# Grouped attention: key blocks stored and loaded by SyncE, both halves in one DMA, and the first turn's operands made ready during the projections

## The reference

```python
q = (hidden_states @ Wq.T)...                    # 32 heads of 128, rotated
k_r0 = hidden_states @ Wkr.T                     # rotary half of the keys
c_kv = hidden_states @ Wdk.T                     # latents
k_c = c_kv @ Wupk.T                              # other half of the keys
v = (c_kv @ Wupv.T).reshape(bsz, q_len, KV_HEADS, HEAD_DIM)
...
attn = jax.nn.softmax(scores, axis=-1)           # causal
out = jnp.einsum('bhqk,bhkd->bhqd', attn, v)
return out.reshape(...) @ Wo.T
```

## Time and profile before

| | us |
|---|---|
| median of 3 runs (2343.11 to 2350.22) | 2343.27 |
| the profiled execution, device time | 2351.52 |
| its span, first to last instruction | 2349.8 |
| TensorE busy | 2125.6 (90%) |
| VectorE busy | 1406.4 (60%) |
| ScalarE busy | 1082.5 (46%) |
| GpSimd busy | 835.4 (36%) |

### The profile page before, as it was taken

The page is one execution under the profiler, slowest core; times in us unless marked ns, Lnnn a source line. Parts: engine busy times, 40 slices in busy tenths (PEclk is TensorE's granted clock), DMA queues, the critical chain, the costliest instruction groups (busy, mean ns, idle before and its releaser), DMA issues. The chain is left out here.

```text
span 2349.8 us, 33208 instructions
## 1 busy us (share of the span) xinstructions
PE 2125.6 (90%) x11408; PEld 1456.4 (62%) x11408; DVE 1406.4 (60%) x2597; ACT 1082.5 (46%) x2627; POOL 835.4 (36%) x1060
## 2 busy tenths in 40 slices
PE   5999988878999999999997879999999986899988
PEld 3333356656777777777765656777777674554457
DVE  5788464326656566556554636666666555657756
ACT  4677543214444444444443635555555433335553
POOL 0000101545344444444431035455555313246621
PEclk8999888989999999999999979999999987989999
DMA  3000022751011111111011144444333201543310
GB/s 112 1 1 1 4 90 84 153 128 41 25 53 37 36 54 32 41 54 32 23 41 36 62 103 108 108 108 105 88 98 78 61 23 58 160 91 68 72 33 37
DMA packets 113587, 149.48 MB, mean 64 GB/s; under 512 B 40127, under 2 KB 53567, under 8 KB 111246
## 3 DMA queue, kind: packets, MB, share of 16 engines
q1 hardware_dynamic: 65422, 109.08, 16.4%
q0 software_dynamic: 48000, 38.28, 7.1%
HBM read 86.39 MB, written 27.26 MB: 48 GB/s over the span
## 5 line engine op out<-in xcount | busy, mean ns | idle before, releaser
L1851 POOL TENSOR_TENSOR attn0b_probs<-attn0b_probs,attn0b_recip 128x128 f32<-128x128 f32 (+3 forms) x256 | 192.4, 772 | 223.4 <-DVE attn0b_recip L2090 223.3
L2482 POOL TENSOR_TENSOR attn1a_probs<-attn1a_probs,attn1a_recip 128x128 f32<-128x128 f32 (+3 forms) x256 | 178.9, 720 | 234.8 <-DVE attn1a_recip L2665 234.2
L2538 ACT ACTIVATE attn1a_probs<-attn1a_scores,attn1a_negmax 128x128 f32<-128x128 f32 (+3 forms) x256 | 132.7, 523 | 175.4 <-DVE attn1a_negmax L2651 174.2
L1957 ACT ACTIVATE attn0b_probs<-attn0b_scores,attn0b_negmax 128x128 f32<-128x128 f32 (+3 forms) x256 | 132.6, 523 | 150.0 <-DVE attn0b_negmax L2083 148.8
L1965 ACT ACTIVATE attn0b_probsT<-attn0b_turned 128x128 f32<-128x128 f32 (+3 forms) x128 | 56.0, 437 | 243.3 <-PE attn0b_turned L2231 242.9
L2244 PE MATMUL attn0b_out<-attn0b_probsT,attn0b_v_now 128*128 128x512 f32 x320 | 153.9, 612 | 11.4 <-DVE attn0b_probsT L2097 11.4
L1440 DVE TENSOR_REDUCE attn0a_negmax<-attn0a_by_query 128x2 f32<-128x1024 f32 x128 | 151.9, 1219 | 11.7 <-PE attn0a_by_query L1557 11.7
L2651 DVE TENSOR_REDUCE attn1a_negmax<-attn1a_scores 128x2 f32<-128x256 f32 (+3 forms) x128 | 105.4, 824 | 71.4 <-PE attn1a_scores L2840 71.4
L2083 DVE TENSOR_REDUCE attn0b_negmax<-attn0b_scores 128x2 f32<-128x256 f32 (+3 forms) x128 | 104.8, 819 | 46.9 <-PE attn0b_scores L2220 46.9
L37 PE MATMUL attn0b_aux<-attn0b_wo_hi,attn0b_oT_hi 128*128 128x512 f32 x256 | 125.6, 490 | 1.4 <-DVE attn0b_oT_lo L2101 1.4
L2852 PE MATMUL attn1a_turned<-ident_f,attn1a_probs 128*128 128x128 f32 x640 | 116.1, 280 | 8.7 <-DVE attn1a_probsT L2659 7.3
(11 more groups left out here) (507 smaller groups left out, 6121.2 us busy)
## 6 DMA issues: line engine op xcount, KB each, us to landing
pre<-in_b_o SPq DMA_DIRECT2D x16, 1024.0 KB, 5.3
attn1a_qT<-attn1a_stage SPq DMA_DIRECT2D x128, 128.0 KB, 2.4
attn1a_qT<-attn1a_stage SPq DMA_DIRECT2D x64, 256.0 KB, 3.8
pre<-in_b_q SPq DMA_DIRECT2D x8, 1024.0 KB, 6.1
pre<-in_b_kv SPq DMA_DIRECT2D x5, 1024.0 KB, 7.1
attn0b_vals<-attn0b_v_out SPq DMA_DIRECT2D x16, 256.0 KB, 5.0
attn0b_keys_hi<-attn0b_part_hi POOLq DMA_DIRECT2D x32, 128.0 KB, 4.9
attn0b_keys_lo<-attn0b_part_lo POOLq DMA_DIRECT2D x32, 128.0 KB, 7.6
```

What stands on the lines that cost most here:

```text
L1851: pool.tensor_tensor(x, x, recip[:, r % 2, e:e + 1].broadcast_to([P, (qt + 1) * P]), ALU.mult).then_inc(s_scaled, 1)
L1957: act.activation(probs[:, r % 2, e, 0:width], scores[r % 2][:, e, 0:width], ACT.Exp, bias=negmax[:, r % 2, e:e + 1], accum_out=sums[:, r % ...
L2482: pool.tensor_tensor(x, x, recip[:, r % DEEP, e:e + 1].broadcast_to([P, (qt + 1) * P]), ALU.mult).then_inc(s_scaled, 1)
L2538: act.activation(probs[:, r % DEEP, e, 0:width], scores[r % 2][:, e, 0:width], ACT.Exp, bias=negmax[:, r % 2, e:e + 1], accum_out=sums[:, ...
```

## The change

- Keys lie in one DRAM tensor by pairs of heads, with the high and the low part of a row beside each other. SP stores a block with two DMAs (64 rows, both parts) and loads a head with four per sequence (32 rows, both parts). GpSimd issues none of these any more and waits for neither stored keys nor the buffer.
- `part` has three slots instead of two for each part.
- SP stores key blocks in order between value blocks. After value block 10 it waits for the first half of the values to be stored and loads those of turn 0; after value block 12 it waits for the key blocks up to N1 and loads the keys of turn 0.
- ScalarE and VectorE split weight block 3 ahead of key block R7 instead of ahead of V7. The output weights of turn 0 are split at N4, not at the second tile.
- In SP's order of the turns key loads now stand ahead of value loads and ahead of the output weight load. ScalarE and VectorE wait for stored keys at the first tile.
- SBUF tensors are laid out anew, so that the keys, values and output weights of turn 0 do not lie over tensors still in use.

```diff
@@ -1666,6 +1666,7 @@
     ROUNDS = PAIRS * TILES_ALL
     HEADS_ALL = TURNS * BATCH * G
     LEAD = 5
+    SLOTS = 3
     FIRST, LAST = -LEAD, TILES_ALL + 1
     KV_WEIGHTS = 5
     kinds = [("D", x) for x in range(8)]
@@ -1689,30 +1690,33 @@
     with ExitStack() as ctx:
         n = Names(nc, ctx, prefix)
         dram = lambda name, shape, dt: nc.dram_tensor(f"{prefix}_{name}", shape, dt, kind="Internal").ap()
-        keys_hi, keys_lo = [dram(f"keys_{k}", (TURNS, 2, 2, 32, BATCH * SEQ), F32R) for k in ("hi", "lo")]
+        keys = dram("keys", (KT, 2, 2, 64, 2, BATCH * SEQ), F32)
         vals = dram("vals", (TILES, P, TURNS * HD), F32)
         with ExitStack() as first:
             take_sb = lambda name, shape, dt=F32: first.enter_context(nc.sbuf_tensor(f"{prefix}_{name}", shape, dt))
+            part = take_sb("part", [P, SLOTS, 2, SEQ], F32R)
+            v_out = take_sb("v_out", [P, 2, DIM])
             w_hi, w_lo = take_sb("w_hi", [P, 2, KT, DIM], F32R), take_sb("w_lo", [P, 2, KT, DIM], F32R)
             cT_hi, cT_lo = take_sb("cT_hi", [P, KT, TILES * P], F32R), take_sb("cT_lo", [P, KT, TILES * P], F32R)
             cos_k, sin_k = take_sb("cos_k", [P, SEQ]), take_sb("sin_k", [P, SEQ])
             by_cos, by_sin = take_sb("by_cos", [P, 2, SEQ]), take_sb("by_sin", [P, 2, SEQ])
-            part_hi, part_lo = take_sb("part_hi", [P, 2, SEQ], F32R), take_sb("part_lo", [P, 2, SEQ], F32R)
-            v_out = take_sb("v_out", [P, 2, DIM])
+        probsT = n.sb("probsT", [P, 2, QT, G, P])
+        qT_hi, qT_lo = n.sb("qT_hi", [P, G, BATCH, SEQ], F32R), n.sb("qT_lo", [P, G, BATCH, SEQ], F32R)
+        probs = n.sb("probs", [P, 2, PAIRS, SEQ])
+        oT_hi, oT_lo = n.sb("oT_hi", [P, 2, G, P], F32R), n.sb("oT_lo", [P, 2, G, P], F32R)
         q_cos, q_sin = n.sb("q_cos", [P, 2, SEQ]), n.sb("q_sin", [P, 2, SEQ])
-        qT_hi, qT_lo = n.sb("qT_hi", [P, G, BATCH, SEQ], F32R), n.sb("qT_lo", [P, G, BATCH, SEQ], F32R)
-        kT_hi, kT_lo = n.sb("kT_hi", [P, BATCH, SEQ], F32R), n.sb("kT_lo", [P, BATCH, SEQ], F32R)
+        q_raw = n.sb("q_raw", [P, SEQ])
+        n.sb("end_of_latents", [P, 3 * SEQ])
+        kT = n.sb("kT", [P, 2, BATCH, SEQ], F32R)
         v_now = n.sb("v_now", [P, BATCH, QT, HD])
+        wo_hi, wo_lo = n.sb("wo_hi", [P, G, DIM], F32R), n.sb("wo_lo", [P, G, DIM], F32R)
+        wq_hi, wq_lo = n.sb("wq_hi", [P, KT, G, HD], F32R), n.sb("wq_lo", [P, KT, G, HD], F32R)
+        cos_q, sin_q = n.sb("cos_q", [P, SEQ]), n.sb("sin_q", [P, SEQ])
+        negmax, sums, recip = [n.sb(k, [P, 2, PAIRS]) for k in ("negmax", "sums", "recip")]
+        kT_hi, kT_lo = kT[:, 0], kT[:, 1]
         w_in = [pre[:, :].rearrange("p (k o) -> p k o", k=KT) for pre in m.pre]
-        wo_in, wo_hi, wo_lo = w_in[1], n.sb("wo_hi", [P, G, DIM], F32R), n.sb("wo_lo", [P, G, DIM], F32R)
-        probs = n.sb("probs", [P, 2, PAIRS, SEQ])
-        probsT = n.sb("probsT", [P, 2, QT, G, P])
-        oT_hi, oT_lo = n.sb("oT_hi", [P, 2, G, P], F32R), n.sb("oT_lo", [P, 2, G, P], F32R)
-        negmax, sums, recip = [n.sb(k, [P, 2, PAIRS]) for k in ("negmax", "sums", "recip")]
+        wo_in = w_in[1]
         wq_in = w_in[0].rearrange("p k (g x) -> p k g x", g=G)
-        wq_hi, wq_lo = n.sb("wq_hi", [P, KT, G, HD], F32R), n.sb("wq_lo", [P, KT, G, HD], F32R)
-        q_raw = n.sb("q_raw", [P, SEQ])
-        cos_q, sin_q = n.sb("cos_q", [P, SEQ]), n.sb("sin_q", [P, SEQ])
         scores = [n.ps(f"scores{i}", [P, PAIRS, SEQ]) for i in range(2)]
         turned = n.ps("turned", [P, PAIRS, QT, P])
         aux, out = n.ps("aux", [P, DIM]), n.ps("out", [P, G, P])
...
             n.sem(k) for k in ("proj", "chi", "clo", "krot", "kadd", "phi", "plo", "v")]
-        s_keys = [n.sem("keys_even"), n.sem("keys_odd")]
+        s_keys = [n.sem(f"keys{k}") for k in range(SLOTS)]
...
+        def stored_until(part):
+            return [32 * len([at for at in range(part + 1) if at % SLOTS == k]) for k in range(SLOTS)]
...
+            def store_keys(f):
+                at = PART[f]
+                half, (mt, b) = 0 if f[0] == "R" else 1, divmod(f[1], BATCH)
+                sp.wait_ge(s_plo, at + 1)
+                for s in range(2):
+                    sp.dma_start(keys[mt, s, half, :, :, bass.ts(b, SEQ)],
+                                 part[64 * s:64 * s + 64, at % SLOTS, :, :].bitcast(F32)).then_inc(s_keys[at % SLOTS], 16)
+            def store_values(x):
+                half, t = divmod(x, TILES)
+                sp.wait_ge(s_v, x + 1)
+                sp.dma_start(vals[t, :, bass.ts(half, DIM)], v_out[:, x % 2, :]).then_inc(s_vals[x % 2], 16)
+            def load_keys(i, b):
+                if i >= 1:
+                    sp.wait_ge(s_scores, PAIRS * (TILES * (i - 1) + QT * (b + 1)))
+                for at in range(4):
+                    s, half = divmod(at, 2)
+                    sp.dma_start(kT[32 * at:32 * at + 32, :, b, :].bitcast(F32),
+                                 keys[i // 2, s, half, bass.ts(i % 2, 32), :, bass.ts(b, SEQ)]).then_inc(s_kload[b], 16)
             for x in range(2, KV_WEIGHTS):
                 load_weights(x)
-            for at in range(16):
-                half, t = divmod(at, TILES)
-                if at == TILES:
+            for f in kinds:
+                if f[0] == "V":
+                    store_values(f[1])
+                if f == ("V", 7):
+                    store_keys(("R", 7))
                     load_queries(0)
                     load_outputs(0)
-                sp.wait_ge(s_v, at + 1)
-                sp.dma_start(vals[t, :, bass.ts(half, DIM)], v_out[:, at % 2, :]).then_inc(s_vals[at % 2], 16)
-            for k in range(2):
-                sp.wait_ge(s_vals[k], 16 * 8)
-            sp.wait_ge(s_proj, len(kinds))
-            for i in range(TURNS):
+                elif f[0] == "V" and f[1] < 7:
+                    store_keys(("R", f[1]))
+                elif f[0] == "N":
+                    store_keys(f)
+                if f == ("V", 10):
+                    for stored in s_vals:
+                        sp.wait_ge(stored, 16 * 4)
+                    for b in range(BATCH):
+                        load_values(0, b)
+                elif f == ("V", 12):
+                    for k in range(SLOTS):
+                        sp.wait_ge(s_keys[k], stored_until(PART["N", 1])[k])
+                    for b in range(BATCH):
+                        load_keys(0, b)
+            for stored in s_vals:
+                sp.wait_ge(stored, 16 * 8)
+            for k in range(SLOTS):
+                sp.wait_ge(s_keys[k], stored_until(15)[k])
+            load_queries(1)
+            load_outputs(1)
+            for i in range(1, TURNS):
+                load_keys(i, 0)
                 load_values(i, 0)
                 if i + 1 < TURNS:
                     load_queries(i + 1)
+                load_keys(i, 1)
+                if i + 1 < TURNS:
                     load_outputs(i + 1)
                 load_values(i, 1)
         @block.gpsimd
         def _(pool):
-            def store_keys(f):
-                at = PART[f]
-                kind, (mt, b) = f[0], divmod(f[1], BATCH)
-                half = 0 if kind == "R" else 1
-                for part, keys, done_by in ((part_hi, keys_hi, s_phi), (part_lo, keys_lo, s_plo)):
-                    pool.wait_ge(done_by, at + 1)
-                    for s in range(2):
-                        pool.dma_start(keys[2 * mt:2 * mt + 2, s, half, :, bass.ts(b, SEQ)],
-                                       part[64 * s:64 * s + 64, at % 2, :]).then_inc(s_keys[at % 2], 16)
-
             def add_key(f):
                 at = PART[f]
                 pool.wait_ge(s_krot, 3 * at + 3)
@@ -1824,20 +1863,6 @@
                         query_weights_lo(0, j)
                 if f[0] == "R":
                     add_key(f)
-                    if PART[f] >= 1:
-                        store_keys(ROT_BLOCKS[PART[f] - 1])
-                if f[0] == "N":
-                    store_keys(ROT_BLOCKS[PART[f] - 1])
-            store_keys(ROT_BLOCKS[-1])
-            for k in range(2):
-                pool.wait_ge(s_keys[k], 16 * 4 * 8)
-
-            def load_keys(i, b):
-                if i >= 1:
-                    pool.wait_ge(s_scores, PAIRS * (TILES * (i - 1) + QT * (b + 1)))
-                for kT, keys in ((kT_hi, keys_hi), (kT_lo, keys_lo)):
-                    pool.dma_start(kT[:, b, :], keys[i].rearrange("s h r t -> (s h r) t")[:, bass.ts(b, SEQ)]).then_inc(
-                        s_kload[b], 16)
             def add_rotated(c):
                 pool.wait_ge(s_rope, 3 * c + 3)
@@ -1852,14 +1877,8 @@
                                        ALU.mult).then_inc(s_scaled, 1)
             pool.wait_ge(s_proj, len(kinds))
-            load_keys(0, 0)
-            load_keys(0, 1)
             for at in range(FIRST, LAST + 1):
                 c = at + LEAD
-                if at >= 0 and at % TILES == QT and at // TILES + 1 < TURNS:
```

(25 more changed lines are left out.)

22 lines of the change are left out of this document (12 added, 10 removed).

## The result

Four runs of the changed kernel have a median of 2317.1 us (2313.92 to 2319.84); four of the kernel before, on the same chip, 2346.74 (2343.11 to 2355.12). The ratio is 0.9864, with a 95% interval of 0.9844 to 0.9883: 1.4% faster, some 30 us. The profiled execution took 2316.88 us, with a span of 2315.2 and a mean clock of 0.957 (before: 2351.52, 2349.8 and 0.952).

What follows compares the result with a forecast made beforehand. TensorE, busy 90% of the span, was taken as the bound, with idle time around grouped attention to win: 16.5 + 7.7 + 3.3 + 7.7 = 35.2 us. That gives 2316.3 or 2308.1 by base; 2310 was taken, range 2299 to 2328.

Steps and rivals of the forecast that it cites:

- The slots and the stretch: From key block R6 to the first query projection, 22.6 us lost; stalls on store slots go, gain 16.5 us.
- sum's remainder of 6.1 us: Loss left in the projections: a new 3.6 us wait ahead of V8 and 2.5 us for one slow block.
- the step on the splits: Weight block 3's split ahead of R7: the 7.46 us wait ahead of N0 goes, 3.6 us comes ahead of V8.
- First loads, queries and output weights: Between projections and first turn: 7.7 us from GpSimd freed of loads, 3.3 us from moving the output weights' split.
- The chain's pace: ScalarE's copy, VectorE's rotation, GpSimd's add per query head: 3.84 us apart, copy 4 after 17.7 us, gain 7.7 us.
- Turns: GpSimd's key loads ahead of each scaling move to SP; TensorE's 1.10 us wait goes seven times, gain 7.7 us.
- The rival that another wait would follow: In the turns, another wait replaces the removed one: 7.7 us less gain, 2318 us; chance 0.12.
- Engines as the limit: Rival in the projections: DMA engines, not slots, limit; 12.6 us of the loss stays, about 2323 us; chance 0.16.
- The base: What the 35.2 us are taken from: the profiled execution's 2351.5 gives 2316.3, the median 2343.3 gives 2308.1; 2310 taken.

Runs made afterwards that it cites:

- experiment 2: The kernel before with three key slots instead of two, 2334.99 us, ratio 0.9935; the changed kernel with two instead of three, 2310.9 us, ratio 0.9842.
- experiment 6: The changed kernel with one part taken back each: weight block 3's split at V7, 2312.07 us; first loads late, 2316.6; output weights' split at second tile, 2316.91.
- E0: Not a run: the first output projection on TensorE's timeline; from the first query projection (Q0) to it took 53.4 us before, 42.5 after.
- experiment 5: The kernel before with key loads moved to SP, 2328.56 us; second kernel: also keys laid out by rows of head pairs, stores still on GpSimd, two slots, 2315.09 us.
- experiment 1: The kernel before with GpSimd's key stores and key loads declared float32 on both sides instead of rounded float32; 2349.64 us, ratio 1.0002.

## Why the prediction was right, point by point
**The slots and the stretch, 16.5 against 16.3.** Right in the sum. The cause, ScalarE's wait for a slot, held: both ways of ending it, experiment 2, give the time. The prediction took 3.8 us from the earlier trace rows for the new store and got 3.5. Of its sum's remainder of 6.1 us (3.6 and 2.5), the trace shows 4.22 of wait and a slow block of 444.50 to 448.92, 4.42 us instead of 2.72, so 1.7: together 5.9. The wait is 0.6 longer, 0.5 of it since GpSimd's add of R7 took 1.76 us and not the 1.26 of the earlier trace rows. The block is shorter since its first microsecond still ran at the high level: after the 7.46 us ahead of N0 TensorE started at 0.50. The windows of V8's block (granted clock, DMA share and GB/s last) and GpSimd's add:

```profile
444.50:445.50 1.00, 1.00 (x4) 0.83 (x5) 1.00 (x3) 1.00 (x3) 0.00 (x0) 0.98 0.95 324
445.50:448.50 3.00, 3.00 (x8) 2.31 (x7) 1.26 (x3) 0.18 (x1) 0.00 (x0) 0.50 0.79 210
```
```profile
440.20 1.76 POOL L1852 TENSOR_TENSOR attn0b_by_cos<-attn0b_by_cos,attn0b_by_sin 128x512 f32<-128x512 f32 x1 [6.89 <-DVE attn0b_by_sin L2052]
```

**What the step on the splits had wrong** was the cause it gave. It wrote that with the moved split the 7.46 us wait is gone. Moved back (experiment 6), the wait is 3.32 and the stretch shorter; the move costs 0.9 us. The step worked out the new wait at V8 and never set it against what N0 would have waited without the store stalls.

**First loads, queries and output weights, 11.0 against 10.9.** The chain's pace from the earlier trace rows held: copy 4 at 17.03 (forecast 17.7), first score 8.4 us earlier, at 14.00 (forecast 14 to 15). With the output split back (experiment 6) the stage from Q0 to E0 is 45.5 us: 7.9 of the 10.9 are the chain's (forecast 7.7), 3.0 the output split's (forecast 3.3). That the chain counts and not the first score is what the loads alone show (experiment 5): first score 4.5 us later than in that experiment's second kernel, the same 45.3 us to E0.

**Turns, 7.7 against 7.7.** The 1.10 us are gone in all seven turns, and a turn takes 91.32 us where it took 92.46. The rival that another wait would follow is out: with GpSimd's loads gone alone, the turns took 705.4 us.

**Engines as the limit** fell with experiment 2: the old stores, in their old shape, go through in 61.3 us with a third slot. The changed kernel moves 178 GB/s over the whole of the projections at a share of 0.61, where the earlier trace rows had 0.95 in its fullest two microseconds; how much of that is the shape and how much the packets, the runs don't settle.

**The base, 2310 against 2317.** The sum was right against the profiled execution (2316.3 against 2316.88), and the step that took 2310 was the choice between two bases. (What lies 8 us over the median is that execution's device time of 2351.5; its span of 2349.8, which the prediction names, lies 6.5 over it.) The median of three runs, 2343.3, was low: with more runs the kernel before has medians of 2346.7, 2352.2, 2346.7 and 2346.2. Against 2346.7 the sum gives 2311.5 and the measurement 2317.1, so some 5 of the 35 us were not in the median run. That the parts come out within 0.3 us each is the comparison of the two profiled executions; in the medians the gain is 29.6 us. The likely reading, which the runs don't settle, is that the profiled execution had more of the stalls than most. The stretch shows this spread, with 77.0 us before, 74.1 with only the loads moved, and 69.9 in experiment 1. How much of the last is due to its packets isn't settled.

## What to carry to other kernels
Before a store is moved to another queue, look at the outermost dimension of both its sides: a block stored as 64 or 32 rows landed in 2.4 to 3.5 us from either queue, and with a 2 in front it took some 6 from GpSimd and held up all of SP's queue. Where a wait goes away, work out what each moved step behind it would cost now, for it may have been placed against the old wait. And size a gain that consists of varying stalls against several executions, since one profile can hold more of them than the median run.
